# Routing a mixture of experts in groups of tiles, with slot tables and gathered token rows, and loops written out

## The reference, cut to what matters

```python
C = int(np.ceil(CAP_FRAC * T))                 # 1024 slots for each expert
logits = x @ wr
probs = softmax(logits);  top1 = argmax(probs)
top2 = argmax(where(m1 > 0, -inf, logits))     # m1, m2: one-hot of top1, top2
loc1 = cumsum(m1, axis=0) - 1
loc2 = cumsum(m2, axis=0) - 1 + m1.sum(0)      # second choices queue behind all first ones
m1, m2 = m1 * (loc1 < C), m2 * (loc2 < C)
buf[top1, s1] = x;  buf[top2, s2] = x          # token rows into slots, the rest dropped
y = (relu(buf @ w1 + b1) @ w2 + b2) * 0.8
out = g1 * y[top1, s1] + g2 * y[top2, s2]
```

## Time and profile before

| | |
|---|---|
| median of 3 runs | 2306.34 us (2303.97 to 2306.47) |
| the profiled execution, its own time | 2296.69 us |
| its span | 2294.9 us |
| PE busy | 1966.2 us, 86% |
| DVE busy | 1352.7 us, 59% |
| ACT busy | 1049.8 us, 46% |
| POOL busy | 500.0 us, 22% |

### The profile page before, as it was taken

How to read it: one execution, slowest core, us unless ns; L and a number is a source line. 1 busy time by engine, 2 the same in 40 slices (tenths; PEclk the granted TensorE clock), 3 DMA queues, 4 the chain that set the end, 5 groups by cost and what they waited for, 6 DMA issues and landing times. The chain is left out here.

```text
span 2294.9 us, 42817 instructions
## 1 busy us (share of the span) xinstructions
PE 1966.2 (86%) x13779; PEld 1461.5 (64%) x13779; DVE 1352.7 (59%) x3560; ACT 1049.8 (46%) x2004; POOL 500.0 (22%) x413
## 2 busy tenths in 40 slices
PE   5689999899999989999998999999855009999996
PEld 3456667576666767666675666666543008898996
DVE  2446767566666656666675766766424405766664
ACT  1245556455555656655564665555512003433332
POOL 1102122121202112021212213121020371322232
PEclk8789999999999999999999999999975559999998
DMA  5223341424425142442514243341221434444343
GB/s 167 74 74 116 106 157 61 142 75 131 148 73 177 45 158 68 138 139 75 185 45 158 68 138 120 111 152 63 65 83 35 164 120 123 88 106 93 78 87 69
DMA packets 223378, 245.30 MB, mean 107 GB/s; under 512 B 12650, under 2 KB 214315, under 8 KB 223168
## 3 DMA queue, kind: packets, MB, share of 16 engines
q1 hardware_dynamic: 210832, 226.57, 30.7%
q0 software_dynamic: 12336, 16.10, 4.0%
HBM read 158.24 MB, written 85.33 MB: 106 GB/s over the span
## 5 line engine op out<-in xcount | busy, mean ns | idle before, releaser
L960 DVE TENSOR_REDUCE MX<-bank 128x2 f32<-128x512 f32 x768 | 493.2, 683 | 224.4 <-PE bank L628 223.0
L1187 ACT ACTIVATE PT<-bank 128x512 f32<-128x512 f32 x768 | 416.7, 596 | 214.2 <-PE bank L665 211.6
L628 PE MATMUL bank<-KS,QS 32*128 32x256 f32 (+1 forms) x1536 | 200.3, 340 | 38.0 <-DVE MX L960 25.1
L680 PE MATMUL bank<-PT,VA 128*32 128x256 f32 x3072 | 214.0, 398 | 11.7 <-ACT PT L1187 10.1
L665 PE MATMUL bank<-QM,KS 32*128 32x256 f32 (+1 forms) x1536 | 192.6, 329 | 12.4 <-ACT PT L1187 11.6
L628 PEld LDWEIGHTS bank<-KS,QS 32*128 32x128 f32 (+1 forms) x1536 | 119.3, 192 | 125.7 <-issue 71.8
L1545 ACT ACTIVATE hid<-bank,b1T 128x512 f32<-128x512 f32 x128 | 88.0, 687 | 234.4 <-issue 188.9
L665 PEld LDWEIGHTS bank<-QM,KS 32*128 32x128 f32 (+1 forms) x1536 | 118.6, 189 | 110.3 <-issue 83.6
L1456 POOL DMA_INDIRECT out_dram<-yo,rows x64 | 106.6, 1666 | 291.5 <-DMA out_dram<-yo,rows 136.0
L480 POOL TENSOR_TENSOR rrB<-uwB,cst 128x4 f32<-128x4 f32 x16 | 16.3, 1018 | 593.2 <-DVE uwB L935 593.2
L1512 PE MATMUL bank<-W2h,hTh 128*128 128x256 f32 x512 | 145.4, 284 | 0.0
(11 more groups left out here) (277 smaller groups left out, 3852.3 us busy)
## 6 DMA issues: line engine op xcount, KB each, us to landing
W<-in_L_ffn_w_dram SPq DMA_DIRECT2D x54, 1024.0 KB, 7.5
KS<-k_dram SPq DMA_DIRECT2D x64, 512.0 KB, 4.9
QS<-q_dram SPq DMA_DIRECT2D x64, 512.0 KB, 5.8
xg<-slots_dram SPq DMA_DIRECT2D x18, 520.0 KB, 4.0
slots_dram<-zeros SPq DMA_DIRECT2D x16, 520.0 KB, 4.0
k_dram<-qTQ SPq DMA_DIRECT2D x32, 256.0 KB, 2.4
q_dram<-pTQ SPq DMA_DIRECT2D x32, 256.0 KB, 6.5
k_dram<-PRP SPq DMA_DIRECT2D x32, 256.0 KB, 2.4
```

Of the source, the lines that this page charges most:

```text
L628: x = mm(halves(u)[:, r, :], Q[strip, slot, r * P:(r + 1) * P], K[strip, slot, :], start=True, stop=True)
L680: x = mm(bank[4][SLOT * j:SLOT * (j + 1), 0:D], V[:, kc, n * per:n * per + SLOT], PT[:, n % 8, kc, :], start=kc == 0, stop=kc == 1, tile_p ...
L960: v.tensor_reduce(MX[:, slot % 2, j, :], halves(u), AX, ALU.max, negate=True).then_inc(h.maxed, 1)
L1187: s_.activation(PT[:, n % 8, :, :], halves(2 + n % 2), ACT.Exp, scale=h.scale).then_inc(h.exp, 1)
```

## The change

It does four things.

1. **Routing in groups.** The 32 tiles are routed as 7, 7, 7 and 7 in round 16, 2 in round 17 and 2 at the start of `experts` (`ROUTED_BY`). A thread R joins the others, and the rounds 16 and 17 follow strings of their own, `LATE` and `LAST`. The first choices fill an expert's table from slot 0 up and the second ones from slot 1023 down, so no group needs to know later counts.
2. **Slot tables.** For each group DVE builds two one-hot operands (`A`, from the low part of a slot's number, and `H`, from its high part times the token's number), and PE's product of them, added up in `R.table`, lists for each slot which token is in it. Zeroed slots, payload and scatters are gone.
3. **Gathers.** POOL fetches each unit's token rows by four indirect DMAs with `get`, and its gates by four more from a small table in DRAM. The adds stay.
4. **Both loops are written out.** Every `Fori` becomes Python's `for`.

```diff
+ROUTED_BY = (((0, 7), (7, 7), (14, 7), (21, 7)), ((28, 2),))
...
-    with fori(2, n - 3, 2) as r:
+    for r in range(2, n - 3, 2):
         round_(r, 0)
         round_(r + 1, 1)
     round_(n - 2, 0)
     round_(n - 1, 1, a=False)
-    round_(n, 0, b=False, a=False)
-    round_(n + 1, 1, b=False, p=False, a=False)
+    round_(n, 0, b=False, a=False, order=LATE)
+    round_(n + 1, 1, b=False, p=False, a=False, order=LAST)
...
+def route_tensor(t, R, g, t0, n, cst, ones, bank, A, H):
...
+    t.matmul(bank[:, 0:n * w], cst[:, C_TRI:C_TRI + P], M, start=True, stop=True)
+    t.matmul(bank[:, P:P + n * w], ones, M, start=True, stop=True).then_inc(R.ranked, 1)
...
+    for c in range(2):
+        for k in range(n):
+            x = t.matmul(bank[:, (2 + c) * P:(3 + c) * P], A[:, 2 * k + c, :], H[(2 * k + c) // 4][:, (2 * k + c) % 4, :], start=k == 0, stop=k == n - 1)
+    x.then_inc(R.tabled, 1)
...
+def route_vector(v, R, g, t0, n, cst, logits, bank, A, H):
...
+    for k in range(n):
+        link(tt(R.runs[:, k + 1, :], R.runs[:, k, :], bank[:, P + k * w:P + (k + 1) * w], ALU.add))
...
+    for k in range(0, 2 * n, 4):
...
+    link(tt(A[:, 0:2 * n, :], lo.unsqueeze(2).broadcast_to([P, 2 * n, P]), R.iota[:, :].unsqueeze(1).broadcast_to([P, 2 * n, P]), ALU.is_equal))
...
-    tok_d = scratch["tokens"].rearrange("(b t p) d -> b p t d", p=P, t=2)
+    tok_d = scratch["tokens"].rearrange("(p b t) d -> b p t d", p=P, t=2)
...
-                    sp.dma_start(slots_d[now(sp, e)], zeros[:, :, :].broadcast_to([P, 4, ROW])).then_inc(s_zero, 16)
...
+                        if e >= B - 2:
+                            t.wait_ge(routes.added, routed(e + 2)[-1][0] + 1)
...
+            load_weights(0)
+            sp.dma_start(b1rows[:, :], a["L1_ffn_b1"].rearrange("e (f p) -> (e f) p", p=P)).then_inc(s_b1, 16)
+            sp.wait_ge(s_gates, 1)
+            sp.dma_start(gates_d.rearrange("(p n) i -> p n i", p=P), gates[:, :, :]).then_inc(s_gated, 16)
+            load_weights(1)
...
-            for n in range(NT):
-                g.wait_ge(s_tk[n % RING], 16 * (n // RING + 1))
-                g.wait_ge(s_pay, n + 1)
-                for put in (put1, put2):
-                    g.indirect_dma_start(out=scratch["slots"], out_offset=bass.IndirectOffsetOnAxis(ap=put[:, n:n + 1], axis=0),
...
+            g.wait_ge(s_slots, 1)
+            fetch(tok_d, xg, 0, s_xg)
+            fetch(tok_d, xg, 1, s_xg)
+            g.wait_ge(s_gated, 16)
+            fetch(gates_d, gg, 0, s_gg)
+            fetch(gates_d, gg, 1, s_gg)
+            g.sem_inc(s_adding, 1)
+            for u in range(UNITS):
+                if u + 2 < UNITS:
+                    g.wait_ge(s_xt, u + 1)
+                    fetch(tok_d, xg, u + 2, s_xg)
+                for r in range(HT4):
+                    n = u * HT4 + r
+                    g.wait_ge(s_yv, n + 1)
+                    g.wait_ge(s_add, n * 16 + 16)
...
+                    if r == 0 and u + 2 < UNITS:
+                        g.wait_ge(s_meta, u + 1)
+                        fetch(gates_d, gg, u + 2, s_gg)
...
             turn(0)
...
+            t.wait_ge(s_bt, 2)
...
+            first = list(pieces(0))
+            for n in range(2):
+                split(0, first[n], n + 1)
+            take(0)
+            for n in range(2, 4):
+                split(0, first[n], n + 1)
+            v.wait_ge(s_bt, 1)
+            v.tensor_copy(b1T[:, :, :].rearrange("p e f -> p (e f)"), bank[7][:, 0:NE * FC]).then_inc(s_bt, 1)
```

More of the change, by code:

```diff
@@ L14 @@
+import math
 from contextlib import ExitStack
@@ L144, in layers @@
+def layers(nc, a, out, scratch, sem, ident, ones, cst, logits, bank, routes):
     B, S, D = a["x"].shape
@@ L988, in threads, with routing @@
                         "E": idle(N_EXP), "V": idle(N_VALUE),
-                        "P": lin2(r - 1, 1 - par) if p_ else idle(N_LIN2), "Q": lin1(r + 1, r - 2, par, a_, d_)}
+                        "P": lin2(r - 1, 1 - par) if p_ else idle(N_LIN2), "Q": lin1(r + 1, r - 2, par, a_, d_), "R": routing(r)}
+            def routing(r):
+                work = routed(r)
+                if r == B:
+                    v.wait_ge(h0.st, B * h0.heads)
+                    route_start_vector(v, routes, cst, bank[5])
+                    yield
+                if work:
+                    wait(v, dve, "D2", r - 3, "lg")
+                for g, t0, n in work:
+                    yield from route_vector(v, routes, g, t0, n, cst, logits, bank[5], hot, spots)
             def outputs(part, h, b, bnk, q):
@@ L1309, in lin2, with experts @@
                 yield
-            schedule(s_.Fori, B, threads)
-def experts(nc, a, out, scratch, sem, ident, ones, cst, logits, bank):
+            schedule(B, threads)
+def experts(nc, a, out, scratch, sem, ident, ones, cst, logits, bank, routes):
     B, S, D = a["x"].shape
@@ L1526, in split, with take @@
                 s_.activation(head, W, ACT.Copy).then_inc(s_wh[i], 1)
-            def take(i):
+            def take(u):
+                s_.wait_ge(s_xt, u + 1)
                 for c in range(DC):
-                    s_.activation(xgT[i][0][:, c, :], bank[c][:, :], ACT.Copy).then_inc(s_xh, 1)
+                    s_.activation(xgT[u % 2][0][:, c, :], bank[c][:, :], ACT.Copy).then_inc(s_xh, 1)
+            first = list(pieces(0))
             s_.wait_ge(s_w[0], 32)
-            for piece in pieces(0):
+            for piece in first[0:2]:
@@ L1534, in _ @@
                 split(0, piece)
-            s_.wait_ge(s_xt, 2)
             take(0)
-            with s_.Fori(0, NE // 2) as k:
-                for j in range(4):
-                    u, e, other = k * 4 + j, k * 2 + j // 2, 1 - j // 2
-                    piece = pieces(other)
-                    for f in range(FC):
-                        free = now(s_, u * FC + (f + 1))
-                        wait_first(s_, (s_bt, 1), s_h, u * FC + (f + 1))
-                        s_.wait_ge(s_hl, free)
-                        s_.activation(hid[:, f % 4, :], bank[HB[f % 4]][:, :], ACT.Relu, bias=b1T[:, bass.ds(e, 1), f]).then_inc(s_hid, 1)
-                        if j % 2 == 0 and f % 2:
-                            if f == 1:
-                                s_.wait_ge(s_w[other], (k + (1 if other else 2)) * 32)
-                            split(other, next(piece))
-                    s_.wait_ge(s_xt, u + 3)
-                    take((j + 1) % 2)
+            for piece in first[2:4]:
+                split(0, piece)
@@ new lines, in _ @@
+            s_.wait_ge(s_bt, 2)
+            for u in range(UNITS):
+                e = u // NH
+                nxt = (e + 1) % 2
+                piece = pieces(nxt)
+                for f in range(FC):
+                    k = u * FC + f
+                    s_.wait_ge(s_h, k + 1)
+                    if k >= 4:
+                        s_.wait_ge(s_hl, k - 3)
+                    s_.activation(hid[:, f % 4, :], bank[HB[f % 4]][:, :], ACT.Relu, bias=b1T[:, e, f:f + 1]).then_inc(s_hid, 1)
+                    if u % NH == 0 and f % 2 and e + 1 < NE:
+                        if f == 1:
+                            s_.wait_ge(s_w[nxt], ((e + 1) // 2 + 1) * 32)
+                        split(nxt, next(piece))
+                if u + 1 < UNITS:
+                    take(u + 1)
@@ new lines, in _ @@
+            for _ in route_vector(v, R, LAST_GROUP, T0, NT - T0, cst, logits, bank[0], hot, spots):
+                pass
+            total = R.runs[:, 0, 0:NE]
+            grid = [P, NE, NE]
+            link(tt(second[:, :, :], R.pos[:, :].unsqueeze(1).broadcast_to(grid), total.unsqueeze(2).broadcast_to(grid), ALU.subtract))
+            link(sc(second[:, :, :], second[:, :, :], 0.0, None, ALU.is_ge))
+            wide = [P, 2, NE * NE]
+            flat = lambda x: x.rearrange("p i e h -> p i (e h)")
@@ new lines, in take @@
+            def take(u):
+                for c in range(DC):
+                    v.wait_ge(s_xh, u * DC + c + 1)
+                    v.tensor_tensor(xgT[u % 2][1][:, c, :], bank[c][:, :], xgT[u % 2][0][:, c, :].bitcast(F32), ALU.subtract).then_inc(s_xl, 1)
+            first = list(pieces(0))
+            for n in range(2):
[4 more added lines that the diff above has]
+            v.wait_ge(s_bt, 1)
```

553 lines of the change are left out of this document (300 added, 253 removed).

## The result

Median of the kernel before 2305.5 us (four runs, 2303.97 to 2306.47), of the changed one 2226.03 us (four runs, 2218.5 to 2233.15): ratio 0.9655, 95% interval 0.9621 to 0.969. The forecast was 2195.5 with a range from 2176 to 2236: the sign and most of the mechanism were right, but the gain was 79.5 us and not 110.8.

What follows compares the result with a forecast made beforehand. PE's stream bounds layers and experts, latency chains rounds 16 and 17, with a hole before the experts. -41.3 - 104.5 + 30 + 2 + 3 = -110.8, from 2306.3 to 2195.5 us, range 2176 to 2236.

Steps and rivals of the forecast that it cites:

- The 41.3 us for the loops: Rounds 3 to 14: writing out the layers' loop saves 41.3 us, of which 31.5 show as PE's waits.
- The hole: Last logits' copy to first product with W1: 133.0 us shrinks to 28.5, a gain of 104.5.
- The step list: In the hole: DVE starts at +3.0, slots known +15.5, rows landed +21.8, PE's turn +23.8, first L1500 +28.5.
- +32 forecast: Rounds 16 and 17 grow by +30 and +2 us from the routing put there.
- the +5 of the forecast: Round 16: D2's head outputs wait for the fourth table in bank 5, so the P thread waits, +5 us.
- Two signs that I had named: Round 16 some 118 us long, and DVE busy above 0.8 until part C's maximum.
- my own +30: Round 16 grows by 30 us from routing 28 tiles; ends 19 (all packed) and 59 (nothing hidden).
- +3: Experts grow by 3 us, from 0 to 7, through POOL's last adds; PE's stream stays the same.
- PE's slack of 14 us: Experts: PE feels no POOL lag below about 14 us, as a unit's rows are fetched that much ahead.
- The written-out code starves its engines: Rival, chance 0.04: instructions fetched once cost the engines waits and undo the loops' gain; 2320 us.
- The loop's cost stays: Rival, chance 0.05: the 41 us belong to these rounds, not to the loop's way back; 2237 us.
- POOL becomes the bound: Rival, chance 0.17: in the experts a gather steps 1.84 us, costing 58 us in place of 3; 2250 us.

Runs made afterwards that it cites:

- The kernel with the order alone: Kernel before with the layers' loop written out, its rounds 16 and 17 following LATE and LAST without any R, no routing there: 2276.97 us.
- Four gathers: Changed kernel with gates carried in the token rows, so from unit 2 on POOL gathers four times a unit, not eight: 2197.58 us, ratio 0.9549.
- twelve: Changed kernel with gates gathered twice, into spare buffers nothing reads, twelve gathers a unit not eight: experts 485.9 us (one execution).

## Why the prediction was right, and where it was off

**What bounds the kernel, and the loops.** Right. The 41.3 us for the loops measured 38.2 in the changed kernel and 37.8 alone. A straight round inside the stretch is 97.2 us, but some are 97.5 to 99.4, and round 14 itself is 97.6 with the loop gone, where I had multiplied its 97.14. The hardware loop itself was the cause: written out alone, with the old routing, it gives the same. Nothing is won in the experts, as said, and nothing is lost to code.

**The hole.** The step list was right, and 104.5 became 97.8. The first gather came at +17.4 (1794.84 - 1777.44), where I had the slots known at +15.5: DVE began at +2.5, its small linked instructions took 10.5 us (forecast 10.3), its two waits for PE's products 3.5 (forecast 2.2), and POOL began 1.0 us behind the last of them (not forecast). Rows landed at +28.8, not +21.8: this is the term that was mis-sized. Beside those 1.9 us, the fourth gather was issued 5.0 us behind the first and not 3.8, since the third took 1.95 us, and it landed 6.4 us behind its issue and not 2.43. I had taken both from the scatter, whose queues were quiet; here the weights of expert 1 and the rows of b2 were in flight (345 GB/s in the mean from 1800 to 1811). I had asked of these weights only whether they come late themselves ("nothing, at most 2"), not what they do to the gathers. Moving expert 1's ahead gave 3.3 us back. The wait for b1T came to 4.65 where 4.7 was forecast.

**Rounds 16 and 17.** +32 forecast; +40 in one profile of the changed kernel and +31 in the other. Of these 9 us, 3.6 lie in round 15, which the change does not touch, and 4.5 in round 17 (65.9 us at a granted clock of 0.58, 61.4 at 0.69). So the size was right within that spread. The mechanism was right only in part. Through the round, step by step against the kernel with written-out layers and the old routing: the sum of B2's attention 11.7 us later (forecast 12); from it to the next sum 42.0 against 33.0 (forecast 6 more); to part C's norm 5.1 more (forecast 4); from there to its maximum 2.0 more (not forecast); maximum to part C's last sum 5.6 more (forecast 5). In the second profile the five are 9.4, 9.2, 6.7, 1.5 and 5.7 us. DVE's timeline shows both sums held by a one-hot of a group (L311), not by their own product:

```profile
1620.17 2.03 DVE L311 TENSOR_TENSOR KS<-XBA,r_iota 128x1792 fp32r<-128x1792 f32 x1
1622.61 0.69 DVE L1298 TENSOR_TENSOR PRP<-bank,Y 128x512 f32<-128x512 f32 x1 [0.41 <-DVE KS L311]
...
1662.36 2.02 DVE L311 TENSOR_TENSOR KS<-XBA,r_iota 128x1792 fp32r<-128x1792 f32 x1
1664.64 0.69 DVE L1305 TENSOR_TENSOR X<-bank,XBP 128x512 f32<-128x512 f32 x1 [0.25 <-DVE KS L311]
```

What I had not seen is the order. I charged all to DVE's instructions; some 8 us come from the new string alone. D2 of batch 14 now stands behind part C's maximum, since bank 5 is lent to the routing, and I had counted only the wait for the table there. The kernel with the order alone has no table to wait for, and its P thread already takes 4.4 us more from part C's maximum to its last sum. So the +5 of the forecast met the 5.6 by luck: most of it was the order. The same kernel has 2.7 of the 11.7 us ahead of the first sum, and takes 4.2 us less from that sum to the next. Two signs that I had named did not come: round 16 is 135.6 us long and not 118 (by my own +30 it should have read 123, from the 93.3 before), and DVE is busy 0.74 of the time until part C's maximum, not above 0.8.

**The experts.** Here the forecast failed: +3 was +24.1. The step is the length of a unit on POOL, 2 x (1.84 + 4 x 1.28) + 2 x 4.63 = 23.2 us, with 1.1 us more allowed for work held up. It measured 25.7. The two stretches with gathers took 7.6 and 7.8 us for the 6.96 of the sum, 1.5 more together: eight gathers at 1.11 + 0.30 and not 1.28 are 1.0 of that, two longer adds part of the rest. The two chained adds took 5.1 and 5.2 for 4.63, 1.0 more together; I had that row from the last add of all, when nothing else was under way, and among the units some wait far longer for the add before (8.9 us at most). So against the 23.2 the gather is 1.0 of 2.5 us. I had allowed for 0.6 of it, and of my own range of 0 to 7 us for the kernel I took the middle. The formula itself holds: with 25.7 it gives 14 x (25.7 - 23.43) - 4.9 = 27 us for the 24.1 measured. PE's slack of 14 us was used up in six units, as 25.7 - 22.76 a unit would have it. I had weighed this as a rival, at a step of 1.84 and 0.17; the truth lay between the two cases, where a unit on POOL has no margin over PE's. To put chances on two points where the cost is a straight line with a bend was the mistake. Four gathers, eight and twelve show the bend.

Why is a gather longer? 16 gathers that met no instruction of DVE took 1.04 us in the mean: half of the 0.13 over my 1.28 is the gather's own. Eleven of the 116 in that stretch took 1.31 to 1.56, ten of them beside a split of the weights on DVE, a subtraction that reads two tiles of SBUF. But 21 others met such a split and were not so long. What decides is the moment. Here a subtraction, then a cast, runs on DVE while POOL begins a gather:

```profile
1959.93 1.22 DVE L1788 TENSOR_TENSOR W1l<-W,W1h 128x1024 fp32r<-128x1024 f32 x1
```

```profile
1959.15 1.07 POOL L1629 DMA_INDIRECT xg<-tokens_dram,get  x1 [0.31 <-issue]
1960.53 1.51 POOL L1629 DMA_INDIRECT xg<-tokens_dram,get  x1 [0.30 <-issue]
```

```profile
1983.91 0.43 DVE L1810 CAST hTh<-hid 128x512 fp32r<-128x512 f32 x1 [0.22 <-ACT hid L1741]
```

```profile
1984.05 1.24 POOL L1629 DMA_INDIRECT xg<-tokens_dram,get  x1 [0.30 <-issue]
```

The gather ends 0.89 us behind the end of the subtraction (1961.15, 1962.04) and 0.95 behind that of the cast (1984.34, 1985.29). So it is in all nine profiles with gathers. Where a subtraction, cast or scaling with all its inputs in SBUF had begun at least 0.10 us ahead of a gather and ran on for 0.15 us or more, the gather ended 0.88 to 0.97 us behind it, 259 times of 259. Beside 80 instructions in the same position that had an input in PSUM the gathers took 1.01 to 1.09 us, as alone. Where the two begin within 0.1 us of each other, both outcomes occur. So a cast holds a gather up like a subtraction does, and costs less because it is short: 0.43 us against 1.22.

The rule that I had drawn on for copies and scalings in two-port mode, of the Trainium skill, SBUF — State Buffer, Who interferes with whom, agrees with these rows: the gather waits until the cast has ended. So does another sentence of the same section: a DVE instruction with two inputs in SBUF contends with a GpSimd instruction that reads SBUF. All of it is worth 0.07 us a gather in the mean of the changed kernel (1.11 against 1.04), some 0.6 us a unit, which is what I had allowed. No run moved DVE's instructions out of the gathers' way.

**The start.** Not in the forecast: 8.0 and 10.3 us more before round 2's store, from code that the change does not touch there. Whether it is a loss of the changed kernel can't be told from one profile of the kernel before: that execution was 8.8 us below the median of its own kernel. In the profiles, the 47 us by which the first one missed the forecast are the experts (21), rounds 15 to 17 (8), the start (8), the hole (7) and the loops (3). On medians 31 us are missing, which the experts, the hole and the loops make up by themselves; that the start and the rounds then add nothing is what the sums leave, not something measured.

**The rivals.** *The written-out code starves its engines*: excluded, by both loops written out alone. *The loop's cost stays*: excluded. *POOL becomes the bound*: this, at two fifths of its price. It had 0.17, and four, eight and twelve gathers show it.

## What to carry to other kernels

Issue on POOL costs by the instruction, hardly by its bytes: count indirect DMAs by unit and compare their steps, plus the chained ones' landings, with the bound engine's unit before adding any; a small payload goes into the row that is fetched anyway. Where two engines' periods are within 5%, forecast with the slope from the bend on, not with "even". And when new steps are interleaved with old ones on in-order engines, run the new order with the new steps taken out: it is a cost of its own, and a step that looks in the way may be what fills another engine's wait.

## What the runs showed of the hardware

- **The start has more than one length for the same instructions.** In twelve further profiles round 2's store came at 303.1 to 304.9 us (seven) or at 308.9 to 311.3 (five). The granted clock of the first 180 us was 0.81 to 0.82 in the former, but for one with 0.79, and 0.76 to 0.79 in the latter; the kernel before has 301.0 at 0.83. A kernel profiled twice fell into the same of the two each time (309.0 and 311.3; 303.1 and 304.8), kernels with and without the change are in both. Windows of the first 180 us, of the changed kernel and of the one before:

```profile
0.00:180.00 180.00, 124.86 (x629) 85.65 (x630) 62.20 (x161) 47.10 (x95) 19.36 (x25) 0.79 0.32 100
```

```profile
0.00:180.00 180.00, 124.68 (x658) 86.28 (x659) 66.66 (x171) 48.19 (x97) 22.74 (x28) 0.83 0.32 100
```

PE is busy the same 125 us and gets through fewer instructions at the lower clock. What decides the clock there was not tried.
- **A loop's way back costs beyond the wait that it shows.** 31.5 us of PE's waits had no name; 38 came back when the loop went. By the stores of token rows, the five rounds behind a way back took some 38 us more than five others.
- **A gather of 8 bytes a row and one of 1 KB a row take the same 1.1 us of POOL** (1.08 and 1.13). One of 1 KB lands 2.8 to 3.1 us behind its issue on quiet queues (3.9 when its own instruction is held up to 1.96), 6.3 to 6.4 beside the loads of weights.
- **A gather waits for a DVE instruction that works from SBUF and began first**, and ends 0.88 to 0.97 us behind it (259 cases in nine profiles), a cast or scaling as well as a subtraction; one with an input in PSUM does not hold it up (80 cases).
- **PE's unit is 22.76 us in the changed kernel (both profiles) and in the one without round 16's groups, 23.4 in all others**, with the same products. Of the 0.66 us a unit, 0.50 are in the 96 products with W2 (one each 0.114 us and not 0.12) and 0.16 in the 48 with W1, at a granted clock of 1.00 in both. It gave nothing, since POOL was the bound; over 16 units it would be 10 us where PE is (an estimate). What makes it was not tried.
